# FFN end: the last group's mixture loaded in eight portions during the fourth body, and the last quarter's scatters, reloads and casts in two halves

## The reference

```
k = int(EXPERT_CAP * t / NUM_EXPERTS)            # 256 of 1024 tokens for each of 8 experts
probs = softmax(einsum('ntd,de->nte', x, gate_w)) transposed to (n, e, t)
g, m = top_k(probs, k)
xin = x[m]                                        # gather
h = gelu(einsum('nekd,edf->nekf', xin, w1))       # 256 -> 1024
h = einsum('nekf,efd->nekd', h, w2)               # 1024 -> 256
out = zeros.at[flat_idx].add(g[..., None] * h)    # scatter-add, fp32
return out.astype(bfloat16)
...
x = x + attention(xn) + ffn(xn)
```

## Time and profile before

| | us |
|---|---|
| median of 3 runs | 2032.63 |
| lowest and highest run | 2028.50 and 2034.15 |
| the profiled execution | 2034.29 |
| its span, first to last instruction | 2032.5 |
| PE busy | 1913.8 (94%) |
| DVE busy | 1311.2 (65%) |
| ACT busy | 1229.0 (60%) |
| POOL busy | 1025.3 (50%) |
| PE idle ahead of `product2` (L1674), whole span | 22.0 |

### The profile page before, as it was taken

One profiled execution on the slowest core, in us unless ns is written; L12 is line 12 of the kernel. 1 busy time (PEld: TensorE's weight loads), 2 busy tenths in 40 slices (PEclk: granted clock), 3 DMA queues, 4 the chain that ended last, 5 costly groups with the idle time before them and its releaser, 6 DMA issues.

```text
span 2032.5 us, 39422 instructions
## 1 busy us (share of the span) xinstructions
PE 1913.8 (94%) x13728; PEld 1289.4 (63%) x13728; DVE 1311.2 (65%) x2598; ACT 1229.0 (60%) x1959; POOL 1025.3 (50%) x904
## 2 busy tenths in 40 slices
PE   3999989999998999999999999999999999999974
PEld 2566556666666666666666666666666666666643
DVE  5677887878764777765577886555555555555535
ACT  3766656667663666666665666666666666666632
POOL 4454354554533554554555545555454545555432
PEclk7999999999999999999999999999999999999987
DMA  6897885766744555555656667566666666666676
GB/s 166 217 257 199 226 227 172 187 177 180 210 130 122 126 119 115 134 120 117 161 147 168 163 156 173 148 162 168 159 177 150 178 153 164 166 158 173 185 154 197
DMA packets 449036, 338.38 MB, mean 166 GB/s; under 512 B 224645, under 2 KB 430474, under 8 KB 448906
## 3 DMA queue, kind: packets, MB, share of 16 engines
q1 hardware_dynamic: 382474, 252.79, 44.6%
q0 software_dynamic: 49152, 67.14, 17.9%
q10 hardware_dynamic: 17280, 16.78, 2.5%
HBM read 185.61 MB, written 100.66 MB: 141 GB/s over the span
## 4 chain that ended last, share of the span: by engine, by line
PE 56%; DMA 3%; POOL 3%; issue 2%; DVE 2%; SPq 2%; ACT 1%; POOLq 0%; ACTq 0%; DVEq 0%
PE pY L1674 28%; PE pH L1660 28%; POOL acc L1500 2%; SPq L223 2%; DMA stage<-in_w 2%; DMA xg<-table,idx 1%; POOL xg L217 1%; DVE yo L1575 1%; DVE hid L1562 0%; DMA acc<-yo,idx 0%; ACT hid L1520 0%; DVE lmix L1593 0%; ACT gel L1517 0%; DMA lacc<-acc 0%; POOL idx L212 0%
## 5 line engine op out<-in xcount | busy, mean ns | idle before, releaser
L1674 PE MATMUL pY<-w2s,hid 128*128 128x256 f16 x6144 | 757.2, 273 | 22.0 <-DVE hid L1562 18.7
L1660 PE MATMUL pH<-xgT,w1s 128*128 128x512 f16 x3072 | 749.7, 380 | 4.4 <-PEq L319 4.4
L1674 PEld LDWEIGHTS pY<-w2s,hid 128*128 128x128 f16 x6144 | 600.2, 98 | 205.8 <-DVE hid L1562 21.6
L1500 POOL DMA_INDIRECT acc<-yo,idx x256 | 415.5, 1623 | 556.3 <-DVE yo L1575 497.7
L1562 DVE SCALAR_TENSOR_TENSOR hid<-gel,cur,hid 128x512 f16<-128x512 f32 x512 | 382.5, 747 | 379.2 <-ACT hid L1520 315.9
L1517 ACT ACTIVATE gel<-pH,cur 128x512 f32<-128x512 f32 x512 | 350.1, 684 | 395.8 <-PE pH L1660 356.6
L1660 PEld LDWEIGHTS pH<-xgT,w1s 128*128 128x128 f16 x3072 | 301.5, 98 | 261.0 <-issue 9.0
L1520 ACT ACTIVATE hid<-gel,cur 128x512 f16<-128x512 f32 x512 | 369.6, 722 | 16.8
L217 POOL DMA_INDIRECT xg<-table,idx x256 | 285.1, 1114 | 113.6 <-issue 60.3
L1172 PE MATMUL pP<-wkv,xT 128*128 128x512 f16 x768 | 191.1, 386 | 0.0
L683 POOL TENSOR_SCALAR xm<-xring,moments 128x256 f32<-128x256 f32 x128 | 130.6, 1031 | 82.4 <-DVE xhl L941 75.4
(11 more groups left out here) (190 smaller groups left out, 1922.8 us busy)
## 6 DMA issues: line engine op xcount, KB each, us to landing
stage<-in_w SPq DMA_DIRECT2D x160, 512.0 KB, 5.7
xring<-in_x SPq DMA_DIRECT2D x16, 1024.0 KB, 6.5
x2ring<-in_x SPq DMA_DIRECT2D x16, 1024.0 KB, 7.7
table<-xhl SPq DMA_DIRECT2D x32, 512.0 KB, 4.0
acc<-zeros SPq DMA_DIRECT2D x16, 1024.0 KB, 5.1
mix<-x2ring SPq DMA_DIRECT2D x32, 512.0 KB, 2.8
fmix<-mix SPq DMA_DIRECT2D x48, 256.0 KB
facc<-acc SPq DMA_DIRECT2D x48, 256.0 KB
```

The costliest lines, as they stand in the source:

```text
L1500: g.indirect_dma_start(acc, bass.IndirectOffsetOnAxis(ap=idx[q][:, s:s + 1], axis=0), yo[i][:, s, :], None, compute_op=ALU.add).then_inc(a ...
L1660: last = t.matmul(pH[hc % 4][:, :], w[:, aw, c, hc * P:(hc + 1) * P], xgT[i][:, ad, c, :], start=k == 0 and c == 0, stop=k == 2 and c == D ...
L1674: last = t.matmul(pY[s // 2][:, s % 2, :], hid[:, hc % 4, ad, s * P:(s + 1) * P], w[:, aw, hc, :], start=hc == 0 and k == 0 and s % 2 == 0 ...
```

## The change

Four things are done, all at the end of the FFN or for it:
- The load of `lmix` moves from the last body to the fourth (`b` = 3) and is cut into its eight pieces: SP issues two, of 512 KB each, at the end of each quarter, behind that quarter's weight parts. `lmix_in` counts all eight, and DVE waits for all of them once.
- In quarter 3 of the last body the scatters wait in pairs: `s` = 0, 1 for the first `y_done`, `s` = 2, 3 for the second. They count on semaphores of their own, `added_end[0]` and `added_end[1]`. SP reloads pieces 4 and 5 of `lacc` after the first pair has landed and 6 and 7 after the second.
- In that quarter DVE does `weigh` ahead of `finish`.
- The casts of `lacc` are split: DVE does those of the even pieces, ACT those of the odd ones (`cast_last`, a new function), the latter in ACT's stream between the stores.

```
-            lmix_in = event("lmix_in", step=16)
+            lmix_in = event("lmix_in", per=LP, step=16)
+            added_end = [event(f"added_end{i}", step=32) for i in range(2)]
...
-                        if last and q == 0:
-                            sp.dma_start(lmix[:, :, :], last_rows[0]).then_inc(lmix_in, 16)
+                        if isinstance(b, int) and b == G1 - 1:
+                            for i in (2 * q, 2 * q + 1):
+                                sp.dma_start(lmix[:, piece_of(i), :], last_rows[0][:, piece_of(i), :]).then_inc(lmix_in, 16)
...
                 for i in range(LP):
-                    if i % (LP // 2) == 0:
-                        sp.wait_ge(added[2 * i // LP], at(added[2 * i // LP], LAST // 2))
+                    if i == 0:
+                        sp.wait_ge(added[0], at(added[0], LAST // 2))
+                    if i >= LP // 2 and i % 2 == 0:
+                        sp.wait_ge(added_end[i // 2 - 2], at(added_end[i // 2 - 2], 0))
...
                         for s in range(4):
+                            if last and q == 3 and s % 2 == 0:
+                                pool.wait_ge(y_done, at(y_done, 4 * b, 2 * q + s // 2))
                             g.indirect_dma_start(
                                 acc, bass.IndirectOffsetOnAxis(ap=idx[q][:, s:s + 1], axis=0), yo[i][:, s, :], None,
-                                compute_op=ALU.add).then_inc(added[i], 16)
+                                compute_op=ALU.add).then_inc(added_end[s // 2] if last and q == 3 else added[i], 16)
...
+                def cast_last(i):
+                    act.wait_ge(lacc_in[i], at(lacc_in[i], 0))
+                    if i >= 2:
+                        act.wait_ge(ldone, at(ldone, i - 2))
+                    a.activation(lffn[:, i % 2, :, :], lacc[:, piece_of(i), :], ACT.Copy).then_inc(lcast[1], 1)
...
                 for i in range(LP):
+                    if i % 2 == 0:
+                        cast_last(i + 1)
                     store_last(i)
...
-                        if fin:
+                        if fin and not (last and q == 3):
                             finish(b, q)
...
                         else:
+                            finish(b, q)
                             for i in range(LP // 2 - 1):
                                 finish_last(i)
...
                 def finish_last(i):
                     if i == 0:
-                        dve.wait_ge(lmix_in, at(lmix_in, 0))
-                    dve.wait_ge(lacc_in[i], at(lacc_in[i], 0))
-                    v.tensor_copy(lffn[:, i % 2, :, :], lacc[:, piece_of(i), :]).then_inc(lcast, 1)
-                    dve.wait_ge(lcast, at(lcast, i))
+                        dve.wait_ge(lmix_in, at(lmix_in, 0, LP - 1))
+                    if i % 2 == 0:
+                        dve.wait_ge(lacc_in[i], at(lacc_in[i], 0))
+                        if i > 0:
+                            dve.wait_ge(ldone, at(ldone, i - 2))
+                        v.tensor_copy(lffn[:, 0, :, :], lacc[:, piece_of(i), :]).then_inc(lcast[0], 1)
+                    dve.wait_ge(lcast[i % 2], at(lcast[i % 2], i // 2))
```

More of the change, by code:

```diff
@@ L1372, in block_program @@
             fin_done = event("fin_done")
-            lmix_in = event("lmix_in", step=16)
+            lmix_in = event("lmix_in", per=LP, step=16)
+            added_end = [event(f"added_end{i}", step=32) for i in range(2)]
             lacc_in = [event(f"lacc_in{i}", step=16) for i in range(LP)]
-            lcast = event("lcast")
+            lcast = [event(f"lcast{i}") for i in range(2)]
             ldone = event("ldone")
@@ L1495, in body @@
                             gather(pool, b, q + 2)
-                        value = held(pool, at(y_done, 4 * b, 2 * q + 1))
-                        pool.wait_ge(consts, 1)
-                        pool.wait_ge(y_done, value)
+                        if not (last and q == 3):
+                            value = held(pool, at(y_done, 4 * b, 2 * q + 1))
+                            pool.wait_ge(consts, 1)
+                            pool.wait_ge(y_done, value)
                         for s in range(4):
+                            if last and q == 3 and s % 2 == 0:
+                                pool.wait_ge(y_done, at(y_done, 4 * b, 2 * q + s // 2))
                             g.indirect_dma_start(
                                 acc, bass.IndirectOffsetOnAxis(ap=idx[q][:, s:s + 1], axis=0), yo[i][:, s, :], None,
-                                compute_op=ALU.add).then_inc(added[i], 16)
+                                compute_op=ALU.add).then_inc(added_end[s // 2] if last and q == 3 else added[i], 16)
                 run_b(pool, body)
                 for par in range(2):
-                    pool.wait_ge(added[par], at(added[par], LAST // 2))
+                    pool.wait_ge(added[par], at(added[par], LAST // 2 - par))
+                    pool.wait_ge(added_end[par], at(added_end[par], 0))
             @block.scalar
```

## The result

| | us |
|---|---|
| changed kernel, median of 6 runs | 2018.48 (2013.70 to 2022.60) |
| kernel before, median of 6 runs | 2032.17 (2027.19 to 2034.15) |
| ratio | 0.9936, 95% interval 0.9922 to 0.9950 |
| changed kernel, profiled execution (span) | 2022.60 (2020.9) |

The change is a gain of 13.0 us by the ratio (10.2 to 15.9). The forecast was 20.2 us. The median, 2018.48, lies 0.02 us inside the upper end of the stated range, which is luck: the interval of the gain leaves the forecast out.

The account below looks back on a forecast made before the run. PE bounds the kernel (busy 94% of the span), with one 13.8 us wait in the last body and a long end. 15.9 + 0 + 4.3 = 20.2 us off the median of 2032.63 gives 2012.4, range 2008.0 to 2018.5.

Parts of the forecast that it names:

- Part 1: Last body: without the 4 MB load the long quarter's whole excess goes, -15.9 us, bounds 13 and 16.
- Part 2: Fourth body: the same 4 MB, two 512 KB portions per quarter, costs 0 us; DMA share about 0.70.
- The first rival: Fourth body: lateness in proportion to bytes, 2.2 us paid per quarter, +8.8 us, 2021.2; chance 0.10.
- Part 3: End after the last `weigh`: earlier scatters and reloads in halves give -4.3 us, bounds -1.3 to -6.8.
- The start: Last quarter's scatters: first starts 0.9 us earlier, last 1.9 earlier, or 1.0 if the first keeps its 2.50.
- the pitch of 1.86: Last four scatters: starts 1.86 us apart throughout, the first scatter taking 1.56 us instead of 2.50.
- The landing: Last scatter lands 5.2 us after its start, kept because stores of pieces 0 to 3 still lie beside the scatters.
- What follows the landing: Pieces 6 and 7: issued at 16.0, landing at 20.8 and 22.5, last add ending 24.9, span ending 28.2.
- the taking of turns between queues: Reload of pieces 6 and 7: at half rate beside stores, costing 1.7 us instead of 1.1; sum 0.6 less.
- the end gains nothing: End: reloads, scatters and stores share the DMA engines, last store lands as late as before, 2016.7; chance 0.08.
- theory M: From the experiments: DMA engines' work sets the end; 2 MB fewer stores would bring it 4 to 6 us earlier.
- The sum: Whole kernel: 15.9 + 0 + 4.3 = 20.2 us off, giving 2012.4, 1.0% faster.

Follow-up runs that it names:

- only_move: Kernel before with only the `lmix` load moved to the fourth body as eight portions, end as before: ratio 0.9917 (0.9901 to 0.9933).
- finish_first: Changed kernel with DVE's `finish` ahead of the last `weigh` again: ratio 0.9934 (0.9911 to 0.9956).
- late_reload: Changed kernel with pieces 4 to 7 all reloaded after the last pair of scatters: ratio 0.9938 (0.9916 to 0.9960).
- dve_casts: Changed kernel with all casts back on DVE: ratio 0.9913 (0.9883 to 0.9943).
- act_casts: Changed kernel with all casts on ACT, pieces 0 and 1 before the last `weigh`, `finish` behind the adds of 0 and 1: ratio 0.9927 (0.9903 to 0.9951).
- fewer_stores: Changed kernel without the stores of pieces 0 to 3 and SP's wait for them, 2 MB less: ratio 0.9949 (0.9926 to 0.9972).
- hold_dve: Changed kernel with DVE starting its finish, casts and adds only once the last scatters have landed: ratio 0.9929 (0.9912 to 0.9947).
- whole_early_last: Kernel before with its 4 MB `lmix` load ahead of that quarter's sums in the last body: ratio 0.9974 (0.9956 to 0.9992).
- act_casts_late: act_casts with pieces 4 to 7 reloaded after the last pair of scatters: ratio 0.9926 (0.9897 to 0.9955).
- finish_first_late: finish_first with pieces 4 to 7 reloaded after the last pair of scatters: ratio 0.9936 (0.9913 to 0.9959).
- hold_stores: Changed kernel with ACT's stores of pieces 0 to 5 held until the last scatters have landed: ratio 0.9944 (0.9927 to 0.9962).

## Why the prediction was wrong

- **Part 1**, -15.9: right. The long quarter of 36.71 us is 20.84 like the others, which is 15.87, and only_move alone gives 16.9 (13.6 to 20.1). The other 1.0 of the FFN stretch's 16.9 us lies in earlier quarters, within what that stretch varies. The cause, the load ahead of the transposes, was right in mechanism, the late gather included.
- **Part 2**, 0: right. Share of 0.66 to 0.68 against 0.70 forecast, no wait of `product2` in the fourth body. The first rival (2.2 us paid per quarter) didn't come, and even 4 MB at once cost 0.3 us. I had put the safety down to the portions; the gap in the queue was enough.
- **Part 3**, -4.3: wrong. In time after the last `weigh` I had the last scatter start at 7.3, land at 12.5 and the end at 24.7. Measured: 9.56, 17.46, 29.45. The end missed by 4.8 us, of which the start is 2.3, the landing 2.7 and the rest -0.2.
  - *The start.* I took the pitch of 1.86 for all four and read the long first scatter of before as an exception that would go. It was no exception but a rule (below): a scatter that starts beside an add of DVE is longer by what is left of the add. I also priced the move of `finish` behind `weigh` at 0. It made the adds 1.1 us later, onto the second and third scatter, and finish_first shows 1.1 us of start for it. My ground for a short first scatter, that it lies beside `yo`, was no ground: `yo` ends at 1.90, 0.14 us after the scatter's start at 1.76, and a cast of DVE then lengthened it to 1.89.
  - *The landing.* I kept 5.2 us on the ground that the same stores lay beside it, and priced the reload of pieces 4 and 5 only for what it does to later pieces, not for the scatters that it now runs beside. late_reload, with the stores but without that reload, lands after 4.96 us; so the reload is worth 2.9.
  - *What follows the landing* was right: 12.2 us forecast, 12.0 measured, with small errors against each other. The last reload landed 6.0 us after the scatter instead of 6.5, the last store and the rest took 3.6 instead of 3.3. The first of the two pieces landed 3.9 us after its issue. I had 4.8, and 5.4 by the taking of turns between queues that I had weighed. It is no test of that rule, as the stores of pieces 2 and 3, which I put beside this reload, had landed before it was issued.
  - These shares say where the forecast was off, not what each would give back alone: in dve_casts and act_casts an earlier start came back as a longer landing.
- **The rival "the end gains nothing"** (0.08) is what happened, and in part by its reason: the halves do put reload, scatters and stores beside one another, and that is the 2.9 us of landing. The starts are no part of it. Its stricter form, theory M, by which the bytes set the end, is excluded by fewer_stores.
- **The sum.** 16.9 - 0.5 = 16.4 us by the profiles of the two kernels and 13.0 (10.2 to 15.9) by the ratio. So part 3 explains 4.8 of the 7.2 us by which the ratio misses the forecast, and the rest stays open. Nothing in the change touches the stage ahead of the FFN, yet the first `weigh` lies between 661.7 and 670.2 us over the 16 profiles, and that of before is the lowest of them. The single runs of the changed kernel spread over 8.9 us. I take this for that stage's own spread; with one profile of before it isn't shown. only_move's interval overlaps with that of the changed kernel, so neither is shown to be the better.

## What to carry to other kernels

A large prefetch belongs where its issuing queue has nothing due behind it for about as long as it takes to land (here 18 us of 20.7 were enough), and where no other queue has a transfer in that time that somebody waits for closely. Look for that gap in the timeline first. Here, cutting it up was worth nothing where the place was right, and didn't save it where the place was wrong. When an ending is shortened by starting a reload early, price it for the transfers that it now runs beside, since those are still on the chain. Before moving vector work next to GpSimd's indirect DMAs, lay their start times side by side.

## What the runs showed of the hardware

The duration of an indirect DMA's instruction on GpSimd, 1.55 us alone, follows DVE's instructions by two rules that fit all 64 scatters at the end of the sixteen kernels within 0.02 us:
- One that starts while a DVE add of two SBUF tiles runs is longer by what is left of that add less 0.12 us. Before, the first starts at 2.69 with an add until 3.76: 0.95, measured 2.50 - 1.55 = 0.95. dve_casts: start 3.96, add until 4.83, 0.75, measured 0.75. act_casts: start 3.62, add until 4.17, 0.43, measured 0.43. An add that starts after it costs nothing.
- One whose end would fall into a DVE cast from fp32 to bf16 ends 0.08 us behind the cast: the changed kernel's first (cast until 3.56, end 3.65) and second (cast until 6.56, end 6.64). A cast in its middle costs nothing.

Both were read from earlier runs and then gave finish_first's durations, to a tenth, before it ran. The first rule holds beyond the end and beyond adds. Of the 4032 other scatters in the sixteen traces 1082 start beside an operation of DVE that reads two SBUF tiles (the low halves of `hid` and of the weights) with more than 0.12 us of it left. 1048 of these are longer by the same rule, within 0.1 us; in the other 34 the operation had begun at most 0.1 us before the scatter, and they take 1.55 or 1.56 us. Of the 2950 without such a neighbour none takes more than 1.7.

In which instructions interfere, this agrees with the Trainium skill (SBUF — State Buffer, "Who interferes with whom"), by which an instruction with two SBUF inputs contends with GpSimd's reads and a 2-port cast with its port pair. In how, it differs: that section of the Trainium skill says that the loser blocks fully, for the whole instruction, and here only the phase at the scatter's start is exposed to the adds and only that at its end to the casts. I had weighed this in the prediction for one scatter and not for the others.

A scatter of 128 rows lands 3.8 us after its start with nothing beside it (the first three in hold_dve: 3.7 to 3.8). The last of the four lands after 5.0 to 5.8 us with stores (before, only_move, whole_early_last, late_reload, act_casts_late, finish_first_late), 6.1 to 6.8 with the reload of pieces 4 and 5 (hold_stores, hold_dve, fewer_stores), 7.4 to 8.8 with both (the other seven).
